# A message-passing layer on one core: the last tile of seven in eight blocks fetched row by row by SP and ScalarE

## The reference

```python
h = jnp.maximum(_layernorm(x, axis=-1), 0.0)          # (12500, 128)
m_in = jnp.concatenate([h[src], edge_attr], axis=1)   # (400000, 192)
hid = jax.nn.relu(m_in @ msg_w1 + msg_b1)
messages = hid @ msg_w2 + msg_b2
aggregated = jax.ops.segment_sum(messages, dst, num_segments=12500)
u = jax.nn.relu(jnp.concatenate([h, aggregated], axis=1) @ upd_w1 + upd_b1)
out = x + u @ upd_w2 + upd_b2
```

## Time and profile before

| | |
|---|---|
| time, median of 3 runs | 3880.27 us (3878.04 to 3882.97) |
| the profiled execution's own time | 3876.23 us |
| its span in the trace | 3874.4 us |
| mean granted clock of TensorE | 0.733 of full speed |
| busy: PE, VectorE, ScalarE, POOL | 2337.9, 1450.1, 537.4, 2897.5 us |
| DMA: data moved, mean rate | 342.93 MB, 89 GB/s |

### The profile page before, as it was taken

One profiled execution on the slowest core, in us unless ns is written; L12 is line 12 of the kernel. 1 busy time (PEld: TensorE's weight loads), 2 busy tenths in 40 slices (PEclk: granted clock), 3 DMA queues, 4 the chain that ended last, 5 costly groups with the idle time before them and its releaser, 6 DMA issues. The chain is left out here.

```text
span 3874.4 us, 57748 instructions
## 1 busy us (share of the span) xinstructions
PE 2337.9 (60%) x10672; PEld 2015.9 (52%) x10672; DVE 1450.1 (37%) x1593; ACT 537.4 (14%) x630; POOL 2897.5 (75%) x3072
## 2 busy tenths in 40 slices
PE   6587556656666555555655655655655565555555
PEld 4576555545555555544545555545555554455545
DVE  6664333333333333333333333333333333343433
ACT  6321111111111111011111111111111111111111
POOL 7777777777777777777777777777777777777776
PEclk9788776776776777777777667677677777777777
DMA  8233222223222222222322222222232222333322
GB/s 231 89 96 97 79 80 86 80 78 88 79 79 87 79 80 83 83 79 79 88 79 79 87 79 80 81 85 79 79 87 79 80 87 79 99 109 108 111 84 71
DMA packets 168578, 342.93 MB, mean 89 GB/s; under 512 B 80743, under 2 KB 89591, under 8 KB 167883
## 3 DMA queue, kind: packets, MB, share of 16 engines
q0 software_dynamic: 98048, 201.00, 19.4%
q1 hardware_dynamic: 53877, 123.98, 10.0%
q10 hardware_dynamic: 16342, 15.18, 1.4%
HBM read 327.09 MB, written 12.81 MB: 88 GB/s over the span
## 5 line engine op out<-in xcount | busy, mean ns | idle before, releaser
L533 PE MATMUL pre<-w_attr_sb,attrs 128*128 128x256 f32 x3126 | 1262.2, 572 | 1318.7 <-DVE x_all L1033 681.4
L450 POOL DMA_INDIRECT x_all<-table,index x1506 | 1422.6, 945 | 463.4 <-issue 454.2
L450 POOL DMA_INDIRECT rows<-table,index x1486 | 1405.7, 946 | 470.2 <-issue 453.5
L533 PEld LDWEIGHTS pre<-w_attr_sb,attrs 128*128 128x128 f32 x3126 | 857.2, 288 | 1536.7 <-DVE x_all L1033 697.2
L1033 DVE TENSOR_TENSOR x_all<-pre,x_all 128x1024 f32<-128x1024 f32 x192 | 234.6, 1224 | 1078.1 <-DMA x_all<-table,index 943.4
L1033 DVE TENSOR_TENSOR rows<-pre,rows 128x1024 f32<-128x1024 f32 (+1 forms) x190 | 231.6, 1222 | 1015.1 <-DMA rows<-table,index 928.5
L579 PEld LDWEIGHTS seg<-space,rows 128*128 128x128 f32 x3178 | 450.7, 218 | 36.6 <-issue 12.3
L579 PEld LDWEIGHTS seg<-space,x_all 128*128 128x128 f32 x3072 | 439.2, 219 | 31.2 <-issue 11.3
L579 PE MATMUL seg<-space,rows 128*128 128x80 f32 x3178 | 432.5, 296 | 15.7 <-ACT rows L786 7.9
L1087 DVE TENSOR_REDUCE h_space<-space 128x240 f32<-128x1920 f32 x130 | 441.6, 3397 | 0.0
L786 ACT ACTIVATE rows<-rows 128x1024 f32<-128x1024 f32 x199 | 210.0, 1055 | 1558.1 <-DVE rows L1033 1437.0
(11 more groups left out here) (81 smaller groups left out, 556.7 us busy)
## 6 DMA issues: line engine op xcount, KB each, us to landing
attrs<-in_attr SPq DMA_DIRECT2D x130, 768.0 KB
rows<-table ACTq DMA_DIRECT2D x2048, 0.5 KB
rows<-table SPq DMA_DIRECT2D x1920, 0.5 KB
x_all<-table ACTq DMA_DIRECT2D x1920, 0.5 KB
x_all<-table SPq DMA_DIRECT2D x1920, 0.5 KB
x_all<-table,index POOLq DMA_INDIRECT x1506
rows<-table,index POOLq DMA_INDIRECT x1486
table<-rows SPq DMA_DIRECT2D x25, 224.0 KB
```

Of the source, the lines that this page charges most:

```text
L450: pool.indirect_dma_start(slot_rows(j)[:, t, :], None, source, bass.IndirectOffsetOnAxis(index[0:EDGES, j, t:t + 1], 0))\
L533: return pe.matmul(columns(j, q, PAIR)[:, two * 2 * D:(two + 1) * 2 * D], attrs[:, j % 2, start:start + EDGES], w_attr_sb[:, :], start=Tru ...
```

## The change

Three things change. First, seven of the eight slots (all but 4) have their last tile fetched row by row, from round 1 on. Second, each such tile is shared by both queues: rows 0 to 63 are SP's and 64 to 127 ScalarE's. The work of a round is 28 batches of 16 rows per queue, spread evenly: SP's step j has 3 batches for even j and 4 for odd j; ScalarE has one batch behind each relu, and two behind relu 2 of odd j. Third, the row numbers are multiplied once by 512, by VectorE ahead of the edge loop, and the DMAs address `table` as bytes, so that the loaded register is the address; 16 registers are loaded at once.

```diff
-BY_SP = (3, 7)
-BY_ACT = (1, 5)
-BATCH = 8
-BATCHES = P // BATCH
+SINGLE = (5, 6, 7, 0, 1, 2, 3)
+BATCH = 16
+PARTS = 128 // BATCH
+ROW_BYTES = 4 * 128
...
+        table_bytes = table.bitcast(mybir.dt.uint8).rearrange("(a n) d -> a (n d)", a=1)
         fetches = itertools.count()
 
-        def fetch_rows(engine, i, j, slots, part, parts):
-
-            positions = 4 if len(slots) == 2 else 2
-            for s in slots:
-                for k in range(positions):
-                    if (s - 2 - k) % SLOTS != j:
-                        continue
-                    round_of = i + 1 if s - 2 - k < 0 else i
-                    if not single(round_of, s):
-                        continue
-                    target = block_of(round_of, s)
-                    column = (round_of * len(BY_SP + BY_ACT) + (sorted(BY_SP + BY_ACT).index(s) - len(BY_SP + BY_ACT))) * BATCH
-                    each = BATCHES // positions
-                    first = (positions - 1 - k) * each
-                    for n in range(first + part * each // parts, first + (part + 1) * each // parts):
-                        if n == first:
-
-                            engine.wait_ge(hidden_summed, (target - SLOTS) * PAIRS + PAIRS)
-                        site = next(fetches)
-                        registers = [engine.alloc_register(f"row{m}_of_fetch{site}") for m in range(BATCH)]
-                        engine.load(registers, index_rows[n:n + 1, bass.ds(column, BATCH)])
-                        for m in range(BATCH):
-                            p = n * BATCH + m
-                            row = bass.RuntimeValue.of_register_unchecked(registers[m], min_val=0, max_val=N - 1)
-                            engine.dma_start(slot_rows(s)[p:p + 1, TILES_B - 1, :], table[bass.ds(row, 1), :]).then_inc(rows_landed[s], 16)
+        def fetch_rows(engine, half, i, j, part, parts):
+
+
+            each = PARTS // 2
+            total = len(SINGLE) * each
+            step = j * parts + part
+            for m in range(step * total // (SLOTS * parts), (step + 1) * total // (SLOTS * parts)):
+                n, k = divmod(m, each)
+                s = SINGLE[n]
+                round_of = i + 1 if s < SINGLE[0] else i
+                if not single(round_of, s):
+                    continue
+                if k == 0:
+
+                    engine.wait_ge(hidden_summed, (block_of(round_of, s) - SLOTS) * PAIRS + PAIRS)
+                site = next(fetches)
+                registers = [engine.alloc_register(f"row{e}_of_fetch{site}") for e in range(BATCH)]
+                line = n * PARTS + half * each + k
+                engine.load(registers, offsets[line:line + 1, bass.ds((round_of - 1) * BATCH, BATCH)])
+                for e in range(BATCH):
+                    p = (half * each + k) * BATCH + e
+                    offset = bass.RuntimeValue.of_register_unchecked(registers[e], min_val=0, max_val=(N - 1) * ROW_BYTES)
+                    engine.dma_start(slot_rows(s)[p:p + 1, TILES_B - 1, :].bitcast(mybir.dt.uint8), table_bytes[:, bass.ds(offset, ROW_BYTES)])\
+                        .then_inc(rows_landed[s], 16)
...
                 load_attr(i, j)
-                if BY_SP:
-                    fetch_rows(sp, i, j, BY_SP, 0, 1)
+                fetch_rows(sp, 0, i, j, 0, 1)
...
                     relu_hidden(i, j, q)
-                    if BY_ACT:
-                        fetch_rows(act, i, j, BY_ACT, q, PAIRS)
+                    fetch_rows(act, 1, i, j, q, PAIRS)
...
             def edge_loops(wide):
+                dve.wait_ge(row_index_loaded, 16)
+                dve.tensor_scalar(out=offsets[:, :], in0=offsets[:, :], scalar1=float(ROW_BYTES), scalar2=None, op0=ALU.mult)\
+                    .then_inc(offsets_made, 1)
```

More of the change, by code:

```diff
@@ L171, in gnn_layer @@
         rel = sb("rel", [P, PAIR])
-        index_rows = sb("index_rows", [BATCHES, src_rows.shape[1]], I32)
+        offsets = sb("offsets", list(src_rows.shape), I32)
         pre = ps("pre", [P, 2, 1024])
@@ L238, in gnn_layer @@
         index_next_loaded = sem("index_next_loaded")
-        index_rows_loaded = sem("index_rows_loaded")
+        row_index_loaded = sem("row_index_loaded")
+        offsets_made = sem("offsets_made")
         rows_landed = [sem(f"rows_landed{j}") for j in range(SLOTS)]
@@ L297, in single @@
             b = block_of(i, j)
-            return j in BY_SP + BY_ACT and (not isinstance(i, int) or i >= 1) and (not isinstance(b, int) or b < LAST)
+            return j in SINGLE and (not isinstance(i, int) or i >= 1) and (not isinstance(b, int) or b < LAST)
         def landings(i, j, q):
             full = 16 * PAIR
-            if q < PAIRS - 1 or j not in BY_SP + BY_ACT or (isinstance(i, int) and i == 0):
+            if q < PAIRS - 1 or j not in SINGLE or (isinstance(i, int) and i == 0):
                 return i * full + 16 * tiles_of(block_of(i, j), q)
@@ L372, in _ @@
                 sp.dma_start(tile, source).then_inc(w_late_loaded, 16)
-            sp.dma_start(index_rows[:, :], src_rows).then_inc(index_rows_loaded, 16)
+            sp.dma_start(offsets[:, :], src_rows).then_inc(row_index_loaded, 16)
             def load_index(i, j):
@@ L421, in load_block @@
                 load_attr(i, j)
-                if BY_SP:
-                    fetch_rows(sp, i, j, BY_SP, 0, 1)
-            sp.wait_ge(index_rows_loaded, 16)
+                fetch_rows(sp, 0, i, j, 0, 1)
+            sp.wait_ge(offsets_made, 1)
             for k in range(UNROLL):
@@ L813, in relu_block @@
                     relu_hidden(i, j, q)
-                    if BY_ACT:
-                        fetch_rows(act, i, j, BY_ACT, q, PAIRS)
-            if BY_ACT:
-                act.wait_ge(index_rows_loaded, 16)
-                for k in range(UNROLL):
-                    act.wait_ge(table_stored[k], 16 * len(CUT) * GBODIES)
+                    fetch_rows(act, 1, i, j, q, PAIRS)
+            act.wait_ge(offsets_made, 1)
+            for k in range(UNROLL):
+                act.wait_ge(table_stored[k], 16 * len(CUT) * GBODIES)
             for j in range(EARLY, SLOTS):
@@ L1298 @@
     width = attr.shape[2]
-    fetched = [b for b in range(SLOTS, blocks) if b % SLOTS in BY_SP + BY_ACT]
-    edges = np.concatenate([np.arange(EDGES) + (b * TILES_B + TILES_B - 1) * EDGES for b in fetched])
+    rounds = -(-blocks // SLOTS)
+    lines = np.zeros((rounds - 1, len(SINGLE), EDGES), src.dtype)
+    for c, s in enumerate(SINGLE):
+        for i in range(1, rounds):
+            b = i * SLOTS + s
+            if b < blocks:
+                lines[i - 1, c] = src[(b * TILES_B + TILES_B - 1) * EDGES:(b * TILES_B + TILES_B) * EDGES]
     arrays = {
         "x": x,
-        "src_rows": src[edges].reshape(len(fetched), BATCHES, BATCH).transpose(1, 0, 2).reshape(BATCHES, -1),
+        "src_rows": lines.reshape(rounds - 1, len(SINGLE) * PARTS, BATCH).transpose(1, 0, 2).reshape(len(SINGLE) * PARTS, -1),
         "src": src[:body].reshape(blocks, TILES_B, EDGES).transpose(0, 2, 1), "src_last": src[body:].reshape(-1, EDGES).T,
```

## The result

The changed kernel takes 3940.57 us (median of 4 runs, 3939.65 to 3945.12) beside 3879.34 for the kernel before: a ratio of 1.0161, 95% interval 1.0148 to 1.0174. The forecast was 3898 us, in a range from 3825 to 3940, which the result just misses. Its sign and the places of the losses were right; the sum was 43 us short. The profiled execution took 3945.12 us (span 3943.3).

What follows compares the result with a forecast made beforehand. POOL's gathers (1.249 us each) bound nearly everywhere, ScalarE's queue in finishing blocks. From 3876.2: gathers -52.5, idle before block 114 -1.3, start +22.6, finish +40.6, loads +8.4 make 3894; median 4.0 higher: 3898 us, range 3825 to 3940.

Steps and rivals of the forecast that it cites:

- Gathers and steady blocks: GpSimd (POOL): 46 gathers go at 1.249 us each, 57.5 us; steady blocks on SP and ScalarE fit within 28.7 us, costing nothing.
- Price of a row: SP and ScalarE queues: multiplication (37 ns) and one gap go, move stays; 0.39 becomes 0.323 us on ScalarE, 0.41 becomes 0.334 on SP.
- Register load: Loading 16 values instead of 8 adds 0.12 us per batch, upper end 0.35; 70 batches at start and finish make 8.4 us.
- Start: SP's rows delay the attrs loads while the edge pipeline catches up; POOL waits 16.8 and 5.8 us at block 16: +22.6 us, once.
- the landing: At the start, block 15's load of attrs moves for some 5.6 us after SP issues it, read from the DMA share.
- Finish: Blocks 114 to 123: ScalarE's chain takes 32.0 us in even, 38.3 in odd blocks; 319.5 us instead of 278.9, +40.6.
- the cheaper issue: Rival: the move goes too, with its gap; a row is 0.26 us, a batch 5.2; 3832 us, chance 0.15.
- the start without a wait: Rival: POOL's wait at block 16 doesn't form, as PE's 15.8 us may shrink and steps be shorter; 3871 us, chance 0.16.
- Nothing saved per row: Rival: removing the multiplication saves the queues nothing; 0.39 and 0.41 us stay, each batch +1.1 us; 3967 us, chance 0.11.
- 2 us of SP's cover left: Steady blocks: SP needs 20.4 or 26.7 us per block against POOL's 28.7, so no cost.
- The rule of exclusive use: Rival: descriptor generator locked for the whole issue, a row 0.46 us when both queues issue; above 4040 us, chance 0.04.

## Where the prediction was right, and which of its steps failed

- **Gathers and steady blocks**: right. 46 gathers fewer, 1.249 us apart, and not one wait from block 16's second pair to block 114.
- **Price of a row**: right. 37 ns and a gap go, the move stays, the issue keeps 228 and 235 ns; 16 rows take 5.36 us. On SP the forecast's own terms make 0.41 - 0.067 = 0.343 us and not its 0.334; the trace has 0.334 on average at the start, so that slip cost nothing.
- **Register load**: the first step that failed. "Between VectorE's and ScalarE's nothing is seen to grow", and 0.12 us was taken; measured 0.44 to 0.50, above even the stated end of 0.35, and above 1.2 us for a load of 16, which the text had named as a sign of being wrong. VectorE's load of three values (747 ns) was taken as a point on the line of ScalarE's and SP's; on SP itself 4 registers cost 473 ns. On 70 batches this is 31 to 35 us where 8.4 stood.
- **Start**: mechanism right, size 49 instead of 22.6 and some 5 of the load. Block 4's load left at 227.17 and not at 223.5, and SP took 269.9 us from there to block 15's and not 256.3, of which the 38 longer register loads are the greater part (0.46 us each on SP, by the medians of the two kernels). The second step that failed is the landing, "the transfer moves for some 5.6 us": block 15's attrs could be used 16.2 us after the issue. The DMA share says when the bulk moves, and not when the last piece lands; here one sixteenth of the load waited behind the rows of both queues. From there to the end of block 15's first sum it was 14.2 us (15.8 forecast). And the sum had SP as the only keeper: taking all of SP's rows away left waits of 30.8 us, taking ScalarE's away 36.9, both at once none.
- **Finish**: mechanism right, 343.8 us against 319.5. Its 32 batches were each 0.44 to 0.50 us longer by the load (14 to 16 us), the queues' mutual hindrance, which was set at nothing, is some 6.3, and the rest of the cycle is 12.47 and not 12.23 us (2).
- **The rest**, some 7 us: the first gather of the table comes 2.3 us later, block 114 waits 2.55 us and not 0.7, and from block 123 to the end the time stayed at 230 us although two gathers fewer lie there. Start 26.3, finish 24.3, this 7, less the 8.4 already in the sum, make 49 of the 51 us between 3894 and the profiled 3945; 2 us have no place.
- **The rivals**: the cheaper issue and the start without a wait are out. "Nothing saved per row" was priced at 3967; the run that made it true took 4117. Its 2 to 3 us more for each of SP's steps were priced at the ends only, but they carry SP past POOL's 28.7 us in each of the blocks between. "2 us of SP's cover left" was in the text, and was not used there.
- **The rule of exclusive use** (the Trainium skill, Perfetto Trace Analysis, DMA Instruction — HWDGE): between 600 and 3300 us the changed kernel has 178 of ScalarE's batches while SP issues rows too, and they take 5.26 us in the median; with SP's rows taken away it is 5.25. So a lock of the length of an issue is not seen; the hindrance in the finish is some 6.3 us on 32 batches, 0.2 us each.

## What to carry over

Work that one queue does for another engine's sake must be priced where the pipeline has no slack, at its start and end, and for every queue that carries a share: with rows left out there, the same change turned from +1.6% into -1.3%. A small DMA has three prices, the instruction's on the queue, the register load's per value, and the place in the transfers' own line; the last shows in the landing of something else, and only above a rate. When a step's cover is given as 2 us, every rival that lengthens the step by more has to be priced in all the blocks.

## What the runs showed of the hardware

- A register load costs by the register: 4 values take 473 ns (SP), 8 take 737 ns (ScalarE), 16 take 1.16 to 1.29 us; a second load right behind the first is about 0.17 us cheaper (562 for 8).
- Two queues with a 512-byte DMA every 0.33 us each delay other transfers increasingly: a load of 768 KB can be used 6.4 us after its issue and, 200 us later, 19.4. One sixteenth of it is late, eight of 128 packets, and the rows of both queues together move at one per 0.234 us. At 0.40 us each, or with one queue alone, the load is in use after 4.3 to 4.6 us.
- Mean clock and PE's work hardly entered: 0.728 of full speed after, 0.733 before, with PE waiting for its inputs.
